# Two-layer adjacency kernel on one core: transposed adjacency stored by halves, one fetch moved a step earlier, one copy moved behind the exponential

## The reference, cut to what matters

```
# layer 0
diff = (adj[..., None] - mean_relation) ** 2            # 4 kernels
w  = exp(-0.5 * diff / (1e-14 + precision ** 2));  w = w / sum_k(w)
ws = sum over m of w[b, n, m, k]                        # one number a row and kernel
x1 = layernorm(x + concat_k(ws_k * x @ W_k.T))
# layer 1
expert = argmax(mean over rows(x1) @ router_w + router_b)    # one of 4 for each batch
o  = adj @ (x1 @ expert_w[expert])
mean, var of o over all batches with the same expert    # batch norm by expert
out = layernorm(x1 + relu((o - mean) * rsqrt(var + eps) * gamma + beta))
```

## Time and profile before

| | |
|---|---|
| median of three runs | 880.13 us |
| the profiled execution | 878.73 us, its span 876.9 us |
| granted TensorE clock, mean | 0.945 |
| PE, DVE, ACT, POOL busy | 754.6, 754.9, 756.3, 704.8 us |
| DMA | 191.72 MB, mean 219 GB/s |
| steps of layer 0 with layer 1 | about 10.9 us each up to 711 us |
| PE alone on the last z and o units | 711 to 797 us |
| tail | 798 to 877 us |

### The profile page before, as it was taken

One profiled execution on the slowest core, in us unless ns is written; L12 is line 12 of the kernel. 1 busy time (PEld: TensorE's weight loads), 2 busy tenths in 40 slices (PEclk: granted clock), 3 DMA queues, 4 the chain that ended last, 5 costly groups with the idle time before them and its releaser, 6 DMA issues.

```text
span 876.9 us, 12591 instructions
## 1 busy us (share of the span) xinstructions
PE 754.6 (86%) x3922; PEld 356.6 (41%) x3922; DVE 754.9 (86%) x1643; ACT 756.3 (86%) x774; POOL 704.8 (80%) x808
## 2 busy tenths in 40 slices
PE   1444469899999999999999999999999999997772
PEld 1111124344444444444444444444444444444561
DVE  2999988999999999999999999999999992226995
ACT  6999998999999999999999999999999961115983
POOL 6599989899999999999999999999999732003795
PEclk9766669999999999999999999999999999998996
DMA  8899998988797779888987797779887828219999
GB/s 231 209 278 260 213 238 190 217 195 193 193 240 193 193 193 240 193 193 193 239 195 193 193 241 192 193 187 242 197 193 168 158 81 339 96 67 397 342 388 390
DMA packets 251254, 191.72 MB, mean 219 GB/s; under 512 B 210098, under 2 KB 210098, under 8 KB 245170
## 3 DMA queue, kind: packets, MB, share of 16 engines
q1 hardware_dynamic: 251042, 190.90, 81.3%
q10 hardware_dynamic: 144, 0.00, 0.0%
HBM read 91.78 MB, written 48.76 MB: 160 GB/s over the span
## 4 chain that ended last, share of the span: by engine, by line
POOL 35%; DVE 28%; PE 15%; ACT 13%; issue 6%; DMA 2%; SPq 1%; POOLq 0%; DVEq 0%; ACTq 0%
DVE ps_t L1000 12%; DVE wgt L962 11%; PE ps_z L1170 8%; POOL adj_cut L531 7%; POOL x_turn L540 4%; POOL adj_cut L529 4%; POOL adj_in L526 3%; POOL x1p L575 3%; PE ps_o L1188 3%; ACT ps_t L689 3%; ACT ps_t L695 3%; ACT ps_t L693 3%; DVE x_in L984 2%; POOL x_in L566 2%; POOL x_turn L538 2%
## 5 line engine op out<-in xcount | busy, mean ns | idle before, releaser
L1170 PE MATMUL ps_z<-adjT,x1p 128*128 128x512 f16 x1536 | 342.3, 379 | 0.6 <-POOL x1p L575 0.6
L1156 PE MATMUL ps_h<-w0T,x_turn 128*128 128x512 f16 x768 | 194.5, 407 | 74.2 <-DVE x_in L984 63.0
L1000 DVE TENSOR_TENSOR ps_t<-ps_t,wgt 128x1024 f32<-128x1024 f32 x192 | 235.4, 1226 | 16.6 <-ACT ps_t L689 11.7
L962 DVE SCALAR_TENSOR_TENSOR wgt<-wgt,ps_t 128x1024 f32<-128x1024 f32 x192 | 224.7, 1215 | 16.4 <-ACT ps_t L695 16.4
L1170 PEld LDWEIGHTS ps_z<-adjT,x1p 128*128 128x128 f16 x1536 | 150.1, 98 | 182.5 <-POOL x1p L575 2.5
L677 ACT ACTIVATE wgt<-adj_in,neg_mu 128x1024 f32<-128x1024 f32 x192 | 205.7, 1135 | 7.3 <-POOL neg_mu L593 7.3
L683 ACT ACTIVATE wgt<-wgt 128x3072 f32<-128x3072 f32 x64 | 176.5, 2758 | 0.0
L1188 PE MATMUL ps_o<-zT,w_sel 128*128 128x512 f16 x696 | 159.7, 379 | 1.7 <-DMA w_sel<-w_planes 0.9
L1156 PEld LDWEIGHTS ps_h<-w0T,x_turn 128*128 128x128 f16 x768 | 74.9, 103 | 182.4 <-issue 103.2
L531 POOL TENSOR_TENSOR adj_cut<-adj_in,adj_cut 128x1024 f16<-128x1024 f32 x64 | 138.3, 2160 | 5.3
L1188 PEld LDWEIGHTS ps_o<-zT,w_sel 128*128 128x128 f16 x696 | 68.0, 98 | 84.2 <-DMA w_sel<-w_planes 1.4
(11 more groups left out here) (222 smaller groups left out, 810.2 us busy)
## 6 DMA issues: line engine op xcount, KB each, us to landing
adj_in<-in_adj_dram SPq DMA_DIRECT2D x64, 512.0 KB, 4.3
x_in<-in_x_dram SPq DMA_DIRECT2D x64, 256.0 KB, 4.4
x_spill<-x_in SPq DMA_DIRECT2D x28, 512.0 KB, 3.4
out_spill<-o_stage SPq DMA_DIRECT2D x50, 256.0 KB, 3.5
w_sel<-w_planes SPq DMA_DIRECT2D x8, 1024.0 KB, 7.8
adjT<-x_spill SPq DMA_DIRECT2D x6, 1024.0 KB, 8.6
out_dram<-adjT SPq DMA_DIRECT2D x5, 1024.0 KB, 6.3
adjT<-out_spill SPq DMA_DIRECT2D x4, 1024.0 KB, 12.6
```

The source lines that it names most:

```text
L962: v.scalar_tensor_tensor(out=wgt[:, m % 2, j, :], in0=wgt[:, m % 2, j, :], scalar=SUM_SCALE / W0_SCALE, in1=tot, op0=ALU.mult, op1=ALU.mul ...
L1000: v.tensor_tensor(tot, tot, wgt[:, n % 2, j, :], ALU.add).then_inc(dve_tot, 1)
L1156: last = te.matmul(ps_h[:, n % 2, :], xT[:, n % 2, left, c, :], w0T[:, right, c, :], start=(c + i == 0), stop=(c == C - 1 and i == 2))
L1170: last = te.matmul(ps_z[:, u % 2, :], x1p[:, b % 2, left, t, k * P:(k + 1) * P], adjT[:, b % 2, right, t, half * HALF:(half + 1) * HALF], ...
```

## The change

It has four parts.

1. The turned adj is laid out `[P, 2, 2, 2, T, HALF]`: for each buffer first the half of the rows, then the plane. The DMA transposes write the same blocks to other addresses, and the z matmuls read the same 512 columns. Parts 4 and 5 are now the half that the units 56 to 59 read, parts 6 and 7 that of the units 60 to 63.
2. The fetches of o in the tail: o's buffer 4 is fetched when z unit 59 is done (60 units) instead of 63, and that fetch is put ahead of SP's wait for the last unit in fetch_x1(3); the first part of buffer 5 needs only z's last unit, its second part o's last.
3. SP fetches w_sel for batch m in step 8m+12 instead of 8m+13.
4. Of the two z units of step 11, ACT copies the second behind the large exponential (L683) of step 12 instead of next to the first, and DVE makes its low plane in the next step.

```diff
-        adjT = sb("adjT", [P, 2, 2, T, NR], F16)
+        adjT = sb("adjT", [P, 2, 2, 2, T, HALF], F16)
...
+        def z_halves(n):
+
+            return z_unit(n)[:1], z_unit(n)[1:]
...
-                sp.dma_start_transpose(adjT[:, b % 2, :, :, t * P:(t + 1) * P].rearrange("p h t n -> p (h t) n"),
+                sp.dma_start_transpose(adjT[:, b % 2, t // G, :, :, t % G * P:(t % G + 1) * P].rearrange("p h t n -> p (h t) n"),
...
                     elif n == 4:
+                        sp.wait_ge(pe_z, TILES - G)
+                    elif n == 5:
                         sp.wait_ge(pe_z, TILES)
-                    elif n == 5:
-                        sp.wait_ge(pe_o, TILES)
...
                     for h in range(2):
+                        if n == 5 and h == 1:
+                            sp.wait_ge(pe_o, TILES)
                         sp.dma_start(o_buf[i][h], o_lines[b, h]).then_inc(o_back[i], 16)
...
                     if n == 3 and g == 1:
+                        fetch_o(4)
                         sp.wait_ge(pe_z, TILES)
...
-                if u % T == 0 and 0 <= u < TILES:
-                    m = u // T
+                if (u + 1) % T == 0 and 0 <= u + 1 < TILES:
+                    m = (u + 1) // T
...
-                    wait(sp, pe_o, u)
-                    if u == 0:
+                    wait(sp, pe_o, u + 1)
+                    if m == 0:
...
             fetch_x1(3)
-            for n in range(4, RING):
-                fetch_o(n)
-                fetch_x1(n)
+            fetch_x1(4)
+            fetch_o(5)
+            fetch_x1(5)
             fetch_o(6)
...
                 if z_taken_first(n - 1):
-                    take_z(n - 1)
+                    take_z(z_halves(n - 1)[0])
                 take_o(n - 1)
                 if not z_taken_first(n - 1):
-                    take_z(n - 1)
+                    take_z(z_halves(n - 1)[0])
                 if 0 <= n - 1 < TILES:
                     sum_reciprocal(n - 1)
                 if n < TILES:
                     weigh_others(n)
+                    take_z(z_halves(n - 1)[1])
...
-                    for u in z_unit(n - 1):
+                    for u in (*z_halves(n - 2)[1], *z_halves(n - 1)[0]):
                         low_z(u)
```

More of the change, by code:

```diff
@@ L180, in gnn_program @@
         wgt_flat = flat(wgt[:], "a k n")
-        adjT_flat = flat(adjT[:], "a h t n").bitcast(F32)
+        adjT_flat = flat(adjT[:], "a g h t n").bitcast(F32)
         x1p_flat = flat(x1p[:], "a h t n").bitcast(F32)
@@ L232, in y_row @@
             return y_buf[i][t // G][:, t % G, :]
-        early_in = flat(adjT[:, 1], "h t n").bitcast(F32).rearrange("p (e n) -> p e n", e=E)
+        early_in = flat(adjT[:, 1], "g h t n").bitcast(F32).rearrange("p (e n) -> p e n", e=E)
         late_in = flat(w_sel[:], "a c n").bitcast(F32)
@@ L695, in sum_reciprocal, with take_z @@
                 s.activation(tot, tot, ACT.Exp, scale=-1.0).then_inc(act_rec, 1)
-            def take_z(n):
-                for u in z_unit(n):
+            def take_z(units):
+                for u in units:
                     half, k = u % T // G, u % G
@@ L1170, in z_product @@
                         last = te.matmul(ps_z[:, u % 2, :], x1p[:, b % 2, left, t, k * P:(k + 1) * P],
-                                         adjT[:, b % 2, right, t, half * HALF:(half + 1) * HALF],
+                                         adjT[:, b % 2, half, right, t, :],
                                          start=(t + i == 0), stop=(t == T - 1 and i == 2))
```

## The result

| | before | after |
|---|---|---|
| median, run side by side | 880.17 us (8 runs) | 884.77 us (8 runs, 883.34 to 886.85) |
| ratio | | 1.0048, 95% interval 1.0038 to 1.0058 |
| the profiled execution, its span | 878.73, 876.9 us | 883.44, 881.7 us |

The change makes the kernel slower by 4.6 us. I had predicted 879.2 us, no change that can be measured, with a range to 888.0: the time lies in the range, on the side of rival (a), not of the forecast.

A forecast was written before the change was run, and what follows sets the result against it. The ACT-DVE loop and POOL were taken to bound a step together; -1.1 (third z unit) -0.5 (w_sel waits) +0.7 (late loads) = -0.9 us, layout and tail 0, giving 879.2 us on the 880.13 median; range 876.9 to 888.

The forecast's parts named there:

- rival (a): At batch borders, POOL held for adj tile 8m+15 behind w_sel; total +0.5 us at D 6.0, +13.5 at 8.16; chance 0.33.
- Layout: Turned adj: same transpose blocks, same matmul columns and counts, so 0, some tenths possible either way.
- Third z unit: Step 12: ACT's copy finds its unit ready; ACT and DVE gain 1.8 us, POOL 1.1; counted -1.1.
- The gain of the early fetch: PE's wait for w_sel in batch 5's border goes; 0.5 of 0.6 us counted, bounds 0 to 4.2.
- The cost of the early fetch: SP waits for routing with adj tile 8m+15's load queued behind; 0.5 to 1.0 us in all, 0.7 taken, bounds 0 to 15.
- D: SP's issue time of the adj turn right behind w_sel: 4.7 to 6.6 us, middle 5.65, POOL free up to 5.65.
- Rival (b): PE's waits for w_sel are commoner than profiled and also go: -3.0 us in all, 877.1; chance 0.14.
- The tail: Fetches of o moved earlier there change nothing, as engines never wait for a landing: 0, at most 2.6 us gained.
- Rival (c): Tail bound by the DMA engines from 784 us, 3 MB less there counts: up to -2.6 us, 876.6; chance 0.06.
- The rule of the Trainium skill: Adj load behind w_sel and a turn is told as landed after both; by it alone a cost in each batch.

The follow-up runs named there:

- experiment 9: Kernel before with only the w_sel fetch a step earlier, behind both turns (adj and x): 880.10 us beside 879.71, ratio 1.0005.
- experiment 4: Kernel before with only the new layout and the new order of fetches in the tail: 880.32 us beside 880.24, ratio 1.0000.
- experiment 5: Changed kernel with the early w_sel fetch moved behind both turns and the store of o: 877.83 us beside 879.55 before, ratio 0.9980.
- experiment 1: Kernel before with only the w_sel fetch a step earlier: 888.38 us beside 880.24, ratio 1.0085.
- experiment 8: Changed kernel with the early w_sel fetch between the store of o and turn_x: 878.43 us beside 879.71 before, ratio 0.9980.
- experiment 3: Kernel before with only the third z unit copied behind the large exponential: 878.64 us beside 880.24, ratio 0.9982.
- experiment 6: Changed kernel with the next step's adj and x loads put between the routing wait and the fetch: 889.14 us beside 879.55 before, ratio 1.0105.

## Why the prediction was wrong

- **Layout**: 0, measured 0.1 us with the tail, within the interval. Right.
- **Third z unit**: -1.1 with -1.8 as the upper end; measured -1.6 (0.9982, interval 0.9973 to 0.9991). The mechanism was right to the step (11.45 us, predicted 11.4); POOL gained 1.15 us at that place, as predicted (1.1). As the interval reaches from 0.8 to 2.4 us, it does not tell whether the time followed POOL's 1.1 or ACT's 1.8.
- **The gain of the early fetch**: PE's wait for w_sel went, as predicted. I had counted 0.5 us for it; experiment 9 shows 0 (+0.4, interval -0.4 to +1.2). Small, and on the optimistic side.
- **The cost of the early fetch**: this is the step that failed. It ran: "The load lands at 590.82 + 0.75 + 0.45 + 0.65 + 1.35 + 4.25 + D = 598.27 + D. POOL is not held if D is at most 5.65 us. D is the number on which all hangs", and it gave 0.7 us. D was 5.06 to 5.46 in the six batches, a little under the 5.65 of the working and inside the bound, and the sum held: at batch 5, moved with the routing (594.83 + 0.20), it gives 607.65 for the landing with D = 5.17, and POOL took the tile at 608.13 without a wait. But it followed only the first load behind the stand. SP, which issues in program order, had lost about 9 us (the turn issued at 586.46 before goes out at 596.20), and it does not win them back in the next step: there the turn takes 3.73 us instead of the 1.9 of one that has nothing large close ahead, and a store of x is due as well. The second load, 16 to 17.6 us behind the routing, is the one that holds POOL. Continued by the same rows the sum would have said so: from the first load 0.58 + 0.10 (issue and gap) + 0.4 (x) + 3 to 4 (an estimate for a turn with loads ahead of it; the earlier trace rows has one of 3.09) + 0.7 + 1.35 + 0.65 = 7 to 8 us to the second, so some 16 to 17 behind the routing, and with the 4.3 of the earlier trace rows for its landing 20.2 to 21.2, against POOL's wish at 19.9 to 20.9. Even this would be short, as POOL started on the held second loads 4.96 to 5.88 us after their issue. The true cost is 5.9 us in the changed kernel, instead of 0.7. Two readings behind D were loose as well: only six of the seven fetches had 0.79 MB just ahead (the last has no load of x there), and the 3.09 us taken for a turn alone is the longest of its kind; the others whose loads are 6 us old took 1.5 to 2.0.
- **Rival (a)** had the right place (POOL at the borders, for a load of adj) and sign, and the wrong criterion: it "decides from D = 6.0", and D stayed below. It decides by the whole stretch that SP is late. Its instruction is tile 8m+16, not 8m+15, but for batch 3, where both were late, and batch 6, where tile 63 was late by 0.30 us.
- **Rival (b)**, commoner waits for w_sel: wrong. In experiment 9 they are gone and nothing is gained.
- **The tail**: 0, as predicted. The last store of the profile is 4.37 us later, as all before it is (4.38); the fetches that were moved earlier bring nothing (experiment 4: 880.32 beside 880.24). Rival (c) is out.
- **The rule of the Trainium skill** that I weighed (DMA: Bandwidth & Descriptors, Queues, rings and completion order), that a later load behind w_sel and a turn is told as landed only after both, pointed to the right sign. The traces show the delay in two places. The larger is in the issue: SP, held by the large transposes, issues the second load 2.0 to 5.0 us later than before. The smaller comes after it: from the issue of the seven loads that held POOL to POOL's start are 4.56 to 5.88 us, where all 64 loads land in 4.4 in the median (4.3 before), and without that excess most of the waits of 0.5 to 0.8 us would be gone. The second part may be the rule at work, or only a busier moment of the DMA engines; no run separates these, and none tells by which part of the DMA path a transpose is held.

What stays open: why the early fetch costs 8.1 us alone and 5.9 us beside the other parts. The rows show two differences. Without the third unit POOL wants its loads sooner behind the routing: at 12.3 to 12.7 and 19.9 to 20.3 us in experiment 9, at 13.0 to 13.4 and 20.6 to 20.9 in experiment 5. So the first load, issued at nearly the same place, holds POOL in batches 0 to 3 and 6 of experiment 1, and only in 3 and 6 of the changed kernel. And single loads take longer to arrive. This is tile 32 in experiment 1, SP's issue and POOL's start:

```profile
349.78 0.48 SPq L342 DMA_DIRECT2D adj_in<-in_adj_dram  x1
...
356.48 1.05 POOL L526 TENSOR_SCALAR adj_in<-adj_in 128x1024 f32<-128x1024 f32 x1 [2.35 <-DMA adj_in<-in_adj_dram]
```

That is 6.70 us, where the same tile took 4.96 in the changed kernel. How much each of the two is worth, and why this load was slow, is not shown.

## What to carry to other kernels

When a wait is moved up on an engine that issues in order, count how late everything behind it will be until the engine has caught up, and not only the first transfer behind it; each tile that comes out of the queue in that time has its own due time. Keep the same early fetch, but let the long issues that are ready already (here the transpose of adj) go ahead of the wait: experiments 5 and 8 have the fetch within tenths (1.5 us in batch 5 of experiment 5) as early as the changed kernel and gain 6.3 and 5.9 us on it. The version to take is that of experiment 5, 877.83 us, 0.998 of the kernel before (0.9971 to 0.9989); as nearly all of it comes from the third z unit, the simpler kernel of experiment 3 serves as well (0.9982).

## What the runs showed of the hardware

- SP's issue of one and the same transpose (128x16x128) takes 1.92 us with nothing large close ahead (the example of experiments 5 and 8), 3.6 to 4.4 us as the next turn behind w_sel's in the changed kernel, with a load of adj and x just ahead, 5.06 to 5.46 us straight behind w_sel (1 MB) there, and with both w_sel and the loads just ahead 5.4 to 6.4 us in experiment 5, 5.2 to 6.8 in experiment 8 and 6.0 to 7.9 in experiment 6 (batches 0 to 5). The transpose of x (128x8x128) takes 1.26 to 1.30 us straight behind w_sel in all seven batches of experiment 8. So the large transpose, not a transpose as such, is held up by what is ahead, and SP with it.
- SP's issue of a fetch whose address comes from a routed value starts 0.94 to 0.98 us behind the start of DVE's last routing instruction, where SP stands ready (1.2 us in batch 0).
- DVE's split of an expert's weights (128x1024), one and the same instruction at 68 to 70 us, took 3.08 to 3.10 us in the profiles of the changed kernel and of experiments 1 and 6, and 1.38 to 2.23 in the eight others. Nothing here shows why.
